# Spreading the pseudo-inverse iterate onto its block diagonal for four images per VectorE operation instead of two

## The reference

```python
def moore_penrose_pinv(x, iters=6):
    z = jnp.swapaxes(x, -1, -2) / (col * row)
    for _ in range(iters):
        xz = x @ z
        z = 0.25 * (z @ (13.0 * I - xz @ (15.0 * I - xz @ (7.0 * I - xz))))
    return z
...
out = a1 @ a2_inv @ (a3 @ v)
```

## Time and profile before

| quantity | value |
|---|---|
| median of 3 runs | 323.4 us |
| time of the profiled execution | 325.98 us |
| its span (first to last record) | 324.2 us |
| mean granted TensorE clock | 0.991 |
| TensorE matmul busy | 292.5 us (90%) |
| VectorE busy | 192.6 us (59%) |
| ScalarE busy | 147.4 us (45%) |
| GpSimd busy | 35.5 us (11%) |

### The profile page before, as it was taken

One profiled execution on the slowest core, in us unless ns is written; L12 is line 12 of the kernel. 1 busy time (PEld: TensorE's weight loads), 2 busy tenths in 40 slices (PEclk: granted clock), 3 DMA queues, 4 the chain that ended last, 5 costly groups with the idle time before them and its releaser, 6 DMA issues.

```text
span 324.2 us, 6403 instructions
## 1 busy us (share of the span) xinstructions
PE 292.5 (90%) x2060; PEld 199.4 (62%) x2060; DVE 192.6 (59%) x459; ACT 147.4 (45%) x328; POOL 35.5 (11%) x33
## 2 busy tenths in 40 slices
PE   6998999999989989999999998998998789777973
PEld 2574777777534536899899943657884266225640
DVE  4594999884416676478888566273226366233731
ACT  1087767766336144736556424202114257221940
POOL 4400064000100006001111000012210000000000
PEclk9999999999999999999999999999999999997998
DMA  3863300000000000000000013333000000100001
GB/s 86 233 124 87 101 11 2 2 0 2 2 0 0 0 1 2 0 2 0 2 1 0 0 30 77 74 81 74 19 2 2 19 3 0 21 13 5 0 0 51
DMA packets 9384, 9.16 MB, mean 28 GB/s; under 512 B 4079, under 2 KB 8943, under 8 KB 9071
## 3 DMA queue, kind: packets, MB, share of 16 engines
q1 hardware_dynamic: 9096, 8.53, 11.4%
q10 hardware_dynamic: 264, 0.30, 0.3%
HBM read 8.57 MB, written 0.26 MB: 27 GB/s over the span
## 4 chain that ended last, share of the span: by engine, by line
PE 32%; DVE 10%; DMA 4%; issue 4%; ACT 2%; SPq 1%; DVEq 0%; POOLq 0%; ACTq 0%
DMA recA<-rec_a 4%; PE ps L759 4%; PE ps L765 3%; PE ps L528 3%; PE ps L915 2%; PE ps L999 2%; PE ps L1002 2%; PE ps L905 1%; PE ps L897 1%; PE ps L1012 1%; PE ps L776 1%; PE ps L806 1%; PE ps L990 1%; PE ps L1048 1%; DVE arena L1560 1%
## 5 line engine op out<-in xcount | busy, mean ns | idle before, releaser
L528 PE MATMUL ps<-xC,cstb 128*128 128x512 f32 (+3 forms) x130 | 55.3, 552 | 0.6 <-DVE keyi L1688 0.6
L1405 DVE TENSOR_TENSOR arena<-arena 128x512 f32 x72 | 44.3, 685 | 7.8 <-ACT arena L1106 4.6
L1113 ACT ACTIVATE arena<-ps 128x512 f32<-128x512 f32 x72 | 37.7, 603 | 15.7 <-PE ps L585 15.6
L528 PEld LDWEIGHTS ps<-xC,cstb 128*128 128x128 f32 x130 | 22.8, 190 | 23.7 <-issue 23.5
L585 PE MATMUL ps<-cstb,arena 128*128 128x128 f32 x288 | 36.3, 277 | 0.7 <-DVE arena L1405 0.7
L585 PEld LDWEIGHTS ps<-cstb,arena 128*128 128x128 f32 x288 | 31.0, 140 | 9.4 <-DVE arena L1405 8.6
L593 PE MATMUL ps<-arena 128*32 128x256 f32 x288 | 19.2, 385 | 0.0
L1274 ACT ACTIVATE arena<-ps,rmax 128x256 f32<-128x256 f32 x32 | 14.7, 479 | 3.6 <-DVE rmax L1734 3.3
L1298 ACT ACTIVATE arena<-ps,w2c 128x512 f32<-128x512 f32 x16 | 9.7, 687 | 12.5 <-PE ps L1040 12.5
L759 PE MATMUL ps<-arena 128*128 128x160 f32 x96 | 14.5, 304 | 0.3 <-DVE arena L1588 0.3
L506 POOL TENSOR_TENSOR arena<-w32b,cstb 128x1024 f32<-128x1024 f32 x4 | 7.6, 1893 | 57.5 <-PEq L891 45.8
(11 more groups left out here) (374 smaller groups left out, 520.1 us busy)
## 6 DMA issues: line engine op xcount, KB each, us to landing
arena<-rec_a SPq DMA_DIRECT2D x19, 128.5 KB
toepb<-toep SPq DMA_DIRECT2D x1, 1536.0 KB
w32b<-w SPq DMA_DIRECT2D x1, 1225.0 KB
cstb<-cst SPq DMA_DIRECT2D x1, 1044.0 KB
recA<-rec_a SPq DMA_DIRECT2D x4, 128.5 KB
arena<-rec_b SPq DMA_DIRECT2D x19, 16.5 KB
w1b<-moe_w SPq DMA_DIRECT2D x1, 264.0 KB
xC<-x SPq DMA_DIRECT2D x1, 256.0 KB, 2.9
```

What stands on the lines that cost most here:

```text
L528: mm(ps[bank][:, 0:cols], ident if lhs is None else lhs, (xC if rhs is None else rhs)[:, 0:cols], start=True, stop=True)
L1113: af(SQ[:, c].rearrange("p q n -> p (q n)"), ps[c % BI], ACT.Copy).then_inc(S["s_ev"], 1)
L1405: tt_(ST[:, c], hy.unsqueeze(3).to_broadcast([P, PT, 16, 16]), hx.unsqueeze(2).to_broadcast([P, PT, 16, 16]), ALU.mult).then_inc(S["prod"], 1)
```

## The change

At the end of each step, the spread is no longer made after every update. It is made after the updates of pairs 1 and 3 only, each time for the last two pairs (four images, 512 columns), and adds 2 to `y_bd`. What waits for `y_bd` is unchanged. The number of spreads falls from 24 to 12, and the order on VectorE becomes update, update, spread, update, update, spread.

```diff
@@ -1584,10 +1584,12 @@
                     dve.wait_ge(S["wy_mm"], it * 4 + 1 + q)
                     dve.wait_ge(S["rest_set"], it * 4 + 1 + q)
                     stt(Yz[:, b2], wy, 0.25, pR[:, b2], ALU.mult, ALU.add).then_inc(S["v_new"], 1)
-                    dve.wait_ge(S["v_new"], it * 4 + 6 + q)
-                    tt_(dst[:, b2].rearrange("p b (h m) -> p b h m", h=HEADS),
-                        Yz[:, b2, lo:lo + 16].unsqueeze(2).to_broadcast([P, 2, HEADS, 16]), mask8_for(2), ALU.mult
-                        ).then_inc(S["y_bd"], 1)
+                    if q % 2:
+                        b4 = slice(2 * q - 2, 2 * q + 2)
+                        dve.wait_ge(S["v_new"], it * 4 + 6 + q)
+                        tt_(dst[:, b4].rearrange("p b (h m) -> p b h m", h=HEADS),
+                            Yz[:, b4, lo:lo + 16].unsqueeze(2).to_broadcast([P, 4, HEADS, 16]), mask8_for(4), ALU.mult
+                            ).then_inc(S["y_bd"], 2)
```

## The result

The changed kernel takes **327.43 us** (median of 12 runs, 325.77 to 328.80) beside 323.82 us of the kernel before (12 runs, 322.66 to 325.56). The ratio is 1.0105, with a 95% interval of 1.0084 to 1.0125: 3.4 us slower, with 2.7 to 4.1 as its bounds; the two medians lie 3.6 us apart. In a second set of runs it was 1.0129 (1.0094 to 1.0164). The ratios of the later sets leave out three executions of 384 to 492 us, whose mean granted clock was 0.555 to 0.747. I had forecast slower by 2.2 us, in a range of 324.4 to 326.8. The direction was right, the size too small, and the median lies 0.6 us above the range.

The account below looks back on a forecast made before the run. TensorE, without a gap in the loop, was taken as the bound. Loop hand-overs 1.56, first 0.35 and last 0.32 sum to 2.2 us on 323.4, giving 325.6 us, range 324.4 to 326.8.

Parts of the forecast that it names:

- rival A: VectorE's count of operations sets the iteration's pace; twelve merges save 2.3 us, giving 321.1 us; chance 0.04.
- Point 1: Each spread of 512 columns takes 0.69 us instead of 0.425, with bounds 0.43 and 1.43.
- rival D: The wide spread takes 1.43 instead of 0.69 us; six hand-overs lengthen by 4.4 in all, 330 us; chance 0.03.
- Point 2: Loop hand-over: second update 1.03 us after L765's matmuls start (T), update to spread 0.25; 0.29 us of TensorE standstill each.
- rival B: Hand-over slack holds because pair 1's product comes almost with pair 0's; no loop change, 323.8 us; chance 0.08.
- Point 3: TensorE restarting after a wait costs 0.10 us more; bare weight loads would add 0.6 us over seven restarts.
- Point 4: Second wide spread in the loop is hidden with 0.22 us to spare; four loop hand-overs cost 1.56 us.
- Point 5: First hand-over: L759 starts 0.45 us later, 0.10 of waiting for later pairs goes away; net 0.35 us.
- Point 6: Last hand-over, to L796: L796 ends at 184.70 instead of 184.38, 0.32 us.
- rival C: Clock drawn anew after the iteration: low stretch at 294 us falls away (324.1 us, 0.07) or second appears (327.1 us, 0.04).

Follow-up runs that it names:

- spread of eight: Changed kernel with one spread of eight images (1024 columns) behind all four updates; ratio 1.0360 to the kernel before.
- increments of one: Changed kernel with y_bd counted once per four images (increment 1 instead of 2, TensorE's waits adjusted); ratio 1.0085 to the kernel before.
- second half alone: Kernel before with the merge in pairs 2 and 3 only, pairs 0 and 1 spread one by one; ratio 1.0049 to the kernel before.

## Why the prediction was right and wrong

**What bounds the kernel** was right: TensorE in the loop without a gap, so that a late spread costs its lateness in full. The spread of eight confirms it most strongly, and against rival A, the operation count: VectorE's busy time fell with the change from 192.6 to 191.1 us, and the kernel became slower.

**Point 1, the wider spread**: 0.69 us taken, 692 ns measured, all twelve times, which is against rival D. The kernel before already held a spread of 1024 columns that took 1224 ns (L1512), so the 2852 ns of L1496 were no fair bound. **Point 2**: the second update at T+1.03, measured T+1.04, which is against rival B. But I took the distance from update to spread from today's rows, 0.25 us, and it was 0.33. That is the step of the sum that failed. The change adds 2 where 1 was added; that looked like bookkeeping, and I gave it no price. It made the wait a separate instruction in each of the twelve spreads, and that is worth 0.50 us of the iteration. **Point 3**: a restart costs 0.05 us in L759 (2.44 against 2.39), not 0.10. By the Trainium skill ("TensorE: Matmul & The Clock Gate", Part 2, the step on LDWEIGHTS) weight loads are pulled ahead under running matmuls, and from that I had worked out a whole bare load of 0.19 us behind a wait; the trace is further still from that. Point 3 also speaks of seven restarts where my own sum has six. **Point 4**: second half hidden, as said. Together 0.435 us a loop hand-over where I said 0.39.

**Point 5**, the first hand-over: 0.47 us later and 0.15 less in L759, so 0.32 where I said 0.35. **Point 6**, the last: from T to the end of L796 4.33 us instead of 3.83, so 0.50 where I said 0.32; both spreads there carry the late wait. In all, 1.74 + 0.32 + 0.50 = 2.56 against my 2.23, and 2.55 measured. With increments of one it was 2.05, just under the forecast: so luck was in it too, since the separate wait that I left out and the restart that I took too dear partly cancel.

**What put the median outside the range** is more than point 2. The forecast was 325.6 and the median 327.43, 1.8 us more. The kernel before itself is 0.4 us higher in twelve runs than in three, and the iteration is 0.3 us longer than my sum. With these two alone the median would be 323.82 + 2.55 = 326.4, inside the range. The rest, 1.1 us, belongs to no term of the sum. The term that I had put at nothing is the clock inside the iteration, and a low stretch elsewhere I gave one chance in 25.

**The clock, rival C**, was drawn at the wrong place. I wrote that standstills of 0.3 us would not lower it in the iteration. In the loop that held, even with idle times of 1.65 us. But in one profile the low clock came behind the first hand-over. TensorE reaches L759 there 1.04 us later than T+1.73, where it was 0.57 before, and I had priced that at 0.35 us net and nothing more. That the gap causes it is not shown: one profile in five is too few to set against none in five, and the low clock at 213 us had no such gap right ahead of it.

**What stays open.** The standstill gives 2.55 us, and the low clock in step 1 about 0.3 on average. The mean granted clock of the timed runs points the same way: 0.990 and 0.989 for the changed kernel, 0.991 to 0.992 for the kernel before. How much time goes with it can be read from the runs: over the 21 executions of the changed kernel a straight line gives 0.17 us for each 0.001 of clock, over 60 of the kernel before 0.10. So a difference of 0.001 to 0.003 is, by this estimate, 0.1 to 0.5 us. With the standstill that makes 2.7 to 3.1 us. The first interval, 2.7 to 4.1, includes it; the second set, at 4.2 us (3.0 to 5.3), only just. Some 0.5 us of the first set's difference and more of the second's have no cause that these runs show.

**The range** was too narrow for a further reason: it was built from the scatter of three runs (1.0 us). Twelve runs of the same kernel spread by 2.9 us; where the low clock falls is a part of that. For the same reason a single pair of profiles misleads. I expected the profiled execution at 328.2 us, and it took 327.3, below that, although its iteration was 4.22 us longer: the profile of the kernel before had been the longest of its five (324.2 us of span, the others 320.9 to 323.5).

## What to carry to other kernels

Merging operations on an engine that is not the bound saved nothing here, and it delays the first result by the wait for the last input plus the added width; compare that with the room that the first consumer has, here 0.46 us. Do not merge what is consumed first, and before merging what is consumed later, check its room against the consumer's unchanged pace: here the second half alone still cost 0.24 us a step. When an edit turns a semaphore's increment of 1 into 2, look whether the instruction's wait becomes one of its own.

## What was not expected of the hardware

- The spread, a VectorE operation with a wait, had no separate wait instruction when it added 1 to its semaphore; with an increment of 2 the wait was a separate EVENT_SEMAPHORE (12 against 0 of them), and 0.33 us passed from update to spread instead of 0.26.
- Two VectorE operations of which the second depends on the one before it stand 0.25 us apart (a 64-column update ahead of it); with an independent one between, 0.14.
- Behind a wait TensorE took 0.05 us more for L759 (160 columns; 2.44 against 2.39) and 0.10 more for L765 (64 columns; 2.00 against 1.90).
- TensorE kept its full clock for 34 us with an idle time of 1.65 us in each 6.7. In another kernel it lost it once behind an idle time of 0.77 us, in one profile of five of the same code, and once at 213 us, where TensorE had been busy for all but 0.2 of the 8 us before.
